# Single-pass rounded-and-remainder score products in the first attention, stacked by groups of batches, scores three steps ahead

## What is computed

```python
def _L0_xattn_ref(x, context, Wq, bq, Wk, bk, Wv, bv, Wo, bo):   # 16 heads of 8 numbers
    q, k, v = heads(x @ Wq.T + bq), heads(context @ Wk.T + bk), heads(context @ Wv.T + bv)
    attn = softmax(einsum('bhnd,bhmd->bhnm', q, k) * HEAD_DIM ** -0.5)
    return merged(einsum('bhnm,bhmd->bhnd', attn, v)) @ Wo.T + bo
x = x + tanh(g_xattn[0]) * _L0_xattn_ref(_layernorm(x), ctx_1024, ...)
x = x + tanh(g_ffn[0]) * _L0_ffn_ref(_layernorm(x), ...)     # 16 experts, top 4, gated
x = x + tanh(g_xattn[1]) * _L1_xattn_ref(_layernorm(x), ctx_1024, ctx_1024, ...)
x = x + tanh(g_ffn[1]) * _L1_ffn_ref(_layernorm(x), ...)     # butterfly up, gelu, butterfly down
```

## Time and profile before

| | |
|---|---|
| time, median of 3 runs (lowest to highest) | 355.55 us (355.16 to 359.48) |
| the profiled execution's own time; its span | 356.27 us; 354.5 us |
| mean granted TensorE clock | 0.986 |
| TensorE matmul busy | 314.1 us, 89% |
| VectorE busy | 240.3 us, 68% |
| ScalarE busy | 211.8 us, 60% |
| GpSimd busy | 159.5 us, 45% |
| DMA packets | 15,091, 27.93 MB |

### The profile page before, as it was taken

The page is one execution under the profiler, slowest core; times in us unless marked ns, Lnnn a source line. Parts: engine busy times, 40 slices in busy tenths (PEclk is TensorE's granted clock), DMA queues, the critical chain, the costliest instruction groups (busy, mean ns, idle before and its releaser), DMA issues.

```text
span 354.5 us, 7313 instructions
## 1 busy us (share of the span) xinstructions
PE 314.1 (89%) x2654; PEld 222.9 (63%) x2654; DVE 240.3 (68%) x603; ACT 211.8 (60%) x411; POOL 159.5 (45%) x254
## 2 busy tenths in 40 slices
PE   4768998839798998999999978999889998999986
PEld 2435777637677776666666645765656665646866
DVE  5672556625566464969998978788958888758251
ACT  3545366615456576685658666668676566764733
POOL 3358998991998021317936340046200394312020
PEclk9999999969899999999999999999999999999999
DMA  7958220120430004323322223413223332000100
GB/s 232 201 70 186 74 66 4 32 35 4 66 121 7 6 2 138 134 89 112 131 93 87 91 88 86 124 46 108 90 92 115 92 108 97 5 1 3 59 31 30
DMA packets 15091, 27.93 MB, mean 79 GB/s; under 512 B 2552, under 2 KB 4040, under 8 KB 15048
## 3 DMA queue, kind: packets, MB, share of 16 engines
q1 hardware_dynamic: 12720, 23.00, 22.2%
q0 software_dynamic: 1408, 3.18, 4.1%
q10 hardware_dynamic: 928, 1.29, 1.3%
HBM read 24.05 MB, written 1.18 MB: 71 GB/s over the span
## 4 chain that ended last, share of the span: by engine, by line
PE 51%; POOL 14%; DVE 13%; issue 8%; ACT 8%; DMA 5%; SPq 1%; ACTq 0%; DVEq 0%; POOLq 0%
PE bank L1116 10%; PE bank L1105 5%; PE bank L1107 5%; PE bank L1106 5%; PE bank L1226 4%; PE bank L931 4%; PE bank L957 3%; PE bank L1211 3%; DMA x_sb<-in_x 3%; DVE rings L1533 3%; DVE rings L1536 2%; POOL xr L442 1%; POOL w_lo L431 1%; DMA rings<-mxr 1%; ACT rings L792 1%
## 5 line engine op out<-in xcount | busy, mean ns | idle before, releaser
L1105 PE MATMUL bank<-xhl,w_hi 128*128 128x512 f32 x128 | 74.9, 585 | 0.8 <-ACT rings L792 0.8
L792 ACT ACTIVATE rings<-bank,cols 128x512 f32<-128x512 f32 x64 | 44.1, 689 | 49.2 <-PE bank L1107 48.9
L1347 DVE TENSOR_REDUCE nt<-bank 128x4 f32<-128x480 f32 x64 | 39.9, 650 | 40.0 <-PE bank L938 40.0
L1533 DVE SCALAR_TENSOR_TENSOR rings<-rings,gates 128x512 f32<-128x512 f32 x64 | 47.4, 740 | 16.9 <-ACT rings L792 16.6
L1107 PE MATMUL bank<-xhl,w_hi 128*128 128x512 f32 x128 | 50.5, 394 | 0.0
L1106 PE MATMUL bank<-xhl,w_lo 128*128 128x512 f32 x128 | 50.3, 393 | 0.0
L931 PE MATMUL bank<-rings,ks 32*120 32x128 f32 x512 | 38.4, 289 | 10.5 <-DMA rings<-rings 6.4
L796 ACT ACTIVATE rings<-bank,b1c 128x512 f32<-128x512 f32 x64 | 44.0, 688 | 0.5
L931 PEld LDWEIGHTS bank<-rings,ks 32*120 32x120 f32 x512 | 32.3, 186 | 15.9 <-issue 12.4
L938 PE MATMUL bank<-ks,rings 32*128 32x120 f32 x512 | 38.9, 291 | 1.3 <-DVE nt L1347 0.7
L1105 PEld LDWEIGHTS bank<-xhl,w_hi 128*128 128x128 f32 x128 | 24.1, 188 | 18.1 <-ACT rings L792 7.9
(11 more groups left out here) (247 smaller groups left out, 625.9 us busy)
## 6 DMA issues: line engine op xcount, KB each, us to landing
gates<-gate_rows SPq DMA_DIRECT2D x64, 256.0 KB, 3.1
bw<-in_L_ffn_w POOLq DMA_DIRECT2D x4, 512.0 KB, 5.3
x_sb<-in_x SPq DMA_DIRECT2D x4, 256.0 KB, 7.7
x_sb<-in_L_ffn_w SPq DMA_DIRECT2D x2, 512.0 KB, 4.3
wide<-in_ctx ACTq DMA_DIRECT2D x4, 240.0 KB, 6.8
out<-xr SPq DMA_DIRECT2D x3, 256.0 KB, 2.1
gates<-in_flies SPq DMA_DIRECT2D x1, 704.0 KB, 7.0
rings<-rings POOLq DMA_DIRECT2D x8, 64.0 KB, 4.5
```

What stands on the lines that cost most here:

```text
L792: act.activation(esg[:, e % 2, :], SB[1 + e % 2][:, :], ACT.Gelu_apprx_sigmoid, bias=b1_in[:, 0, e:e + 1]).then_inc(s["m_sg"], 1)
L1105: pe.matmul(bk[:, :], w1_hi[:, e, branch, :], low(g), start=True, stop=False)
L1347: dve.tensor_reduce(nt[:, b % 2, OF[n], :], score_bank(b, n)[:, 0:HR * M].rearrange("p (r m) -> p r m", r=HR), AX.X, ALU.max, negate=True) ...
L1533: dve.scalar_tensor_tensor(eq[:, j, :], esg[:, j, :], GELU_LIMIT, gates[:, (n - 1) % NG, :], ALU.min, ALU.mult).then_inc(s["m_eq"], 1)
```

## The change

- **Operands.** The score and turned products of the first attention take float32r operands, for which a product is one MATMUL and one LDWEIGHTS. To keep the precision, each of a head's 8 numbers takes four partitions of the 32: for keys the rounded value, the rounded value again, the remainder and (partition `MAX_ROW`) a one; for queries the rounded value, the remainder, the rounded value again and the maximum or zero.
- **Stacks.** A group of four batches has its own slot of keys and of queries. Slots of groups 0 and 1 lie in `w1_lo` and `w1_hi`, those of 2 and 3 in `ks`, `xhl` and `qs`. A slot is filled by three DMAs for keys and three for queries, each to every fourth partition (32 of them); SP issues all, those of groups 2 and 3 between the `mxr` transfers of steps 0 to 3. GpSimd's `stack` is gone.
- **Remainders.** VectorE makes them (`low_keys`, `low_queries`), eight in all, of float32 from the bank and the rounded row.
- **GpSimd.** It fills the slots of groups 2 and 3 with ones (a CAST of 1920 columns each) and zeros (a MEMSET of 2048 columns each). The splits wait for `st_mm` 32 (the end of the turned products of batches 0 to 7), since `w1_hi` and `w1_lo` hold the slots until then; they stand behind the up bias.
- **Order.** Scores run three steps ahead instead of two. Two more half-phases and `turn_max(1)` stand before step 0; maxima are of b+2 and b+3 in step b.

The diff's core. Left out are the renamed calls of the prologue (`phase(-2, 0)` is now `phase(-3, 0)` and so on), the second attention's tiles `p1`, `p1t` and `hid` that move into `mats`, GpSimd's memsets of slots 0 and 1, and on ScalarE the bitcasts to F32R, `turned_max(b + 2)` and its earlier share of the query stacks.

```diff
@@ -57,6 +57,8 @@
+    MAX_ROW = 3
+    AHEAD = 3
@@ -122,7 +124,17 @@
-        qs = ring_row[:, 0:8 * GT].rearrange("p (i r t) -> p i r t", i=2, r=HR)
+        w1_hi_row = w1_hi[:, :, :, :].rearrange("p e j c -> p (e j c)")
+        w1_lo_row = w1_lo[:, :, :, :].rearrange("p e j c -> p (e j c)")
+        KSLOT, QSLOT = HR * GB * M, HR * GT
+        k_rows = (w1_lo_row[:, 0:KSLOT], w1_lo_row[:, KSLOT:2 * KSLOT], ks[:, 0, :], ks[:, 1, :])
+        q_flat = (w1_hi_row[:, 0:QSLOT], w1_hi_row[:, QSLOT:2 * QSLOT],
+                  xhl[:, :, :].rearrange("p s c -> p (s c)"), qs[:, :])
+        k_slot = [v.rearrange("p (r u m) -> p r u m", r=HR, u=GB) for v in k_rows]
+        q_slot = [v.rearrange("p (r u t) -> p r u t", r=HR, u=GB) for v in q_flat]
+        q_lo = ring_row[:, 0:2 * GT].rearrange("p (i t) -> p i t", i=2)
+        k_lo = ring_row[:, 2 * GT:2 * GT + 2 * GB * M].rearrange("p (i t) -> p i t", i=2)
+        kt_row = ring_row[:, 4 * GT:4 * GT + G * GB * M].rearrange("p (g t) -> p g t", g=G)
@@ -234,17 +245,8 @@
-        def stack_k(eng, g, groups):
-            for i in groups:
-                eng.dma_start(ks[32 * i:32 * i + HD, g % 2, :, :],
-                              kt_row[32 * i:32 * i + 32, g, :]
-                              ).then_inc(s[f"ks_ld{g}"], 16)
...
-        def stack_q(eng, g, groups):
-            for i in groups:
-                eng.dma_start(qs[32 * i:32 * i + HD, g % 2, :, :],
-                              q_rows[g][32 * i:32 * i + 32, :]
-                              ).then_inc(s[f"qs_ld{g}"], 16)
+        def stacked(eng, slot, row, src, landed):
+            eng.dma_start(slot[row:P:4].bitcast(F32), src).then_inc(s[landed], 16)
@@ -265,31 +267,46 @@
-            sp.wait_ge(s["ks_fill"], 1)
-            sp.wait_ge(s["kt_rdy"], 1)
-            stack_k(sp, 0, range(HG))
+            def stack_k(g):
+                if g < 2:
+                    sp.wait_ge(s["ks_fill"], g + 1)
+                else:
+                    sp.wait_ge(s["kb_fill"], g - 1)
+                sp.wait_ge(s["kt_rdy"], g + 1)
+                stacked(sp, k_slot[g], 0, kt_row[:, g, :], f"ks_ld{g}")
+                stacked(sp, k_slot[g], 1, kt_row[:, g, :], f"ks_ld{g}")
+                sp.wait_ge(s["kl_rdy"], g + 1)
+                stacked(sp, k_slot[g], 2, k_lo[:, g % 2, :], f"ks_ld{g}")
...
+            def stack_q(g):
+                sp.wait_ge(s["qs_zero"], g + 1)
+                sp.wait_ge(s["qt_rdy"], g + 1)
+                stacked(sp, q_slot[g], 0, q_rows[g], f"qs_ld{g}")
+                stacked(sp, q_slot[g], 2, q_rows[g], f"qs_ld{g}")
+                sp.wait_ge(s["ql_rdy"], g + 1)
+                stacked(sp, q_slot[g], 1, q_lo[:, g % 2, :], f"qs_ld{g}")
...
+            stack_k(0)
...
-            sp.wait_ge(s["qs_zero"], 1)
-            sp.wait_ge(s["qt_rdy"], 1)
-            stack_q(sp, 0, range(HG // 2))
-            sp.wait_ge(s["ks_fill"], 2)
-            sp.wait_ge(s["kt_rdy"], 2)
-            stack_k(sp, 1, range(HG))
+            stack_q(0)
+            stack_k(1)
...
-            sp.wait_ge(s["qs_zero"], 2)
-            sp.wait_ge(s["qt_rdy"], 2)
-            stack_q(sp, 1, range(HG))
+            stack_q(1)
...
-                sp.dma_start(qs[HD:P:32, (b // GB) % 2, :, b % GB * P:(b % GB + 1) * P], mxr[:, b % 2, :]
+                sp.dma_start(q_slot[b // GB][MAX_ROW:P:32, :, b % GB, :].bitcast(F32), mxr[:, b % 2, :]
...
+                if b in (0, 2):
+                    stack_k(2 + b // 2)
+                if b in (1, 3):
+                    stack_q(2 + b // 2)
@@ -423,6 +440,10 @@
+            for g in range(2, G):
+                pool.tensor_copy(k_rows[g], which[:, MAX_ROW:MAX_ROW + 1].to_broadcast([P, KSLOT])).then_inc(s["kb_fill"], 1)
+                pool.memset(q_flat[g].bitcast(F32), 0.0).then_inc(s["qs_zero"], 1)
@@ -433,9 +454,6 @@
-            split(0)
-            split(1)
@@ -451,25 +469,15 @@
-            def stack(g):
-                pool.wait_ge(s["ks_fill"], 2)
-                pool.wait_ge(s["kt_rdy"], g + 1)
-                pool.wait_ge(s["qt_rdy"], g + 1)
-                pool.wait_ge(s["st_mm"], (g - 1) * GB * HG)
-                stack_k(pool, g, range(HG))
-                stack_q(pool, g, range(HG))
-                pool.dma_start(qs[HD:P:32, g % 2, :, :], qs[HD + 1:P:32, g % 2, :, :]
-                               ).then_inc(s[f"qs_ld{g}"], 16)
...
-            stack(2)
-            split(2)
-            split(3)
-            stack(3)
...
+            def halves():
+                pool.wait_ge(s["st_mm"], 2 * GB * HG)
+                for q in range(NQ):
+                    split(q)
@@ -488,6 +496,7 @@
+            halves()
@@ -859,7 +866,7 @@
-                    pe.wait_ge(s["kt_rdy"], g)
+                    pe.wait_ge(s["kl_rdy"], g)
@@ -888,7 +895,7 @@
-                    pe.wait_ge(s["qt_rdy"], g)
+                    pe.wait_ge(s["ql_rdy"], g)
@@ -908,41 +915,39 @@
-                ahead = b + 2
+                ahead = b + AHEAD
...
-                    i, mc, tc = rows_of(b)
+                    k_, q_, u = k_slot[b // GB], q_slot[b // GB], b % GB
...
-                    ia, ma, ta = rows_of(ahead)
+                    ka, qa, ua = k_slot[ahead // GB], q_slot[ahead // GB], ahead % GB
...
-                        pe.wait_ge(s[f"ks_ld{ahead // GB}"], 16 * HG)
-                        pe.wait_ge(s[f"qs_ld{ahead // GB}"], 16 * (HG + ahead // (2 * GB)))
+                        pe.wait_ge(s[f"ks_ld{ahead // GB}"], 16 * 3)
+                        pe.wait_ge(s[f"qs_ld{ahead // GB}"], 16 * 3)
...
-                            mm = pe.matmul(turned_bank(b, gg)[0:M, r * P:(r + 1) * P], ks[32 * gg:32 * gg + 32, i, r, mc],
-                                           qs[32 * gg:32 * gg + 32, i, r, tc], start=True, stop=True)
+                            mm = pe.matmul(turned_bank(b, gg)[0:M, r * P:(r + 1) * P], k_[32 * gg:32 * gg + 32, r, u, :],
+                                           q_[32 * gg:32 * gg + 32, r, u, :], start=True, stop=True)
...
-                            mm = pe.matmul(score_bank(ahead, n)[:, r * M:(r + 1) * M], qs[rows32, ia, r, ta],
-                                           ks[rows32, ia, r, ma], start=True, stop=True)
+                            mm = pe.matmul(score_bank(ahead, n)[:, r * M:(r + 1) * M], qa[rows32, r, ua, :],
+                                           ka[rows32, r, ua, :], start=True, stop=True)
...
-                need(pe, "x1_rdy", b - 3)
+                need(pe, "mxr_rdy", b)
+                need(pe, "x1_rdy", b - 4)
@@ -1045,8 +1050,11 @@
+            phase(-2, 1)
+            phase(-1, 0)
+            turn_max(1)
...
-            pe.wait_ge(s["kt_rdy"], G)
+            pe.wait_ge(s["kl_rdy"], G)
@@ -1058,8 +1066,8 @@
-                if b + 1 < NB:
-                    turn_max(b + 1)
+                if b + 2 < NB:
+                    turn_max(b + 2)
@@ -1275,8 +1283,22 @@
-            keys_of = which[:, HD:HD + 1].unsqueeze(2).to_broadcast([P, HR, GB * M])
-            dve.tensor_copy(ks[:, 0, :, :], keys_of).then_inc(s["ks_fill"], 1)
+            keys_of = which[:, MAX_ROW:MAX_ROW + 1].to_broadcast([P, KSLOT])
+            dve.tensor_copy(k_rows[0], keys_of).then_inc(s["ks_fill"], 1)
...
+            def low_keys(g):
+                dve.wait_ge(s["kt_rdy"], g + 1)
+                if g >= 2:
+                    dve.wait_ge(s[f"ks_ld{g - 2}"], 16 * 3)
+                dve.scalar_tensor_tensor(k_lo[:, g % 2, :].bitcast(F32R), bank[4][:, 0:GB * M], bcol[:, CK0:CK0 + 1],
+                                         kt_row[:, g, :], ALU.add, ALU.subtract).then_inc(s["kl_rdy"], 1)
...
+            def low_queries(g):
+                dve.wait_ge(s["qt_rdy"], g + 1)
+                if g >= 2:
+                    dve.wait_ge(s[f"qs_ld{g - 2}"], 16 * 3)
+                dve.scalar_tensor_tensor(q_lo[:, g % 2, :].bitcast(F32R), bank[2][:, :], bcol[:, CQ0:CQ0 + 1],
+                                         q_rows[g], ALU.add, ALU.subtract).then_inc(s["ql_rdy"], 1)
@@ -1320,16 +1342,24 @@
-            dve.tensor_copy(ks[:, 1, :, :], keys_of).then_inc(s["ks_fill"], 1)
+            dve.wait_ge(s["ld_kb"], 16)
+            low_keys(0)
+            dve.tensor_copy(k_rows[1], keys_of).then_inc(s["ks_fill"], 1)
...
+            low_keys(1)
...
-            for g in range(1, G):
-                normed_rows(g)
+            normed_rows(1)
+            low_queries(0)
+            low_keys(2)
+            normed_rows(2)
+            normed_rows(3)
+            low_queries(1)
+            low_keys(3)
@@ -1421,19 +1451,23 @@
+            low_queries(2)
+            low_queries(3)
...
+            for n in range(HG):
+                maxima(1, n)
...
-                maxima(1, n)
+                maxima(2, n)
...
-                if b + 1 < NB:
-                    maxima(b + 1, HG - 1)
+                if b + 2 < NB:
+                    maxima(b + 2, HG - 1)
...
-                if b + 2 < NB:
```

(3 more changed lines are left out.)

43 lines of the change are left out of this document (19 added, 24 removed).

## The result

The changed kernel takes 369.99 us (median of 4 runs, 369.13 to 372.71); the kernel before, beside it, 357.51 us (4 runs, 355.16 to 360.74). The ratio is 1.0385, with a 95% interval of 1.0275 to 1.0494: slower, where 346.7 us and a gain had been forecast. The profiled execution took 369.65 us, with a span of 367.8.

A forecast was written before the change was run, and what follows sets the result against it. Bound: a step loop through TensorE and VectorE, plus stalls costing 10.2 us. With start +6.4 and 0.44 saved per step, GpSimd binds: mark −9.2, half-phase −0.44, clock +0.8, sum −8.8: 347.4 profiled, 346.7 median; range 342 to 354.

The forecast's parts named there:

- (d): Start: TensorE waits longer before step 0 and its clock is halved after the wait; 0.5 us allowed.
- half chance +0.8: Behind TensorE's wait for GpSimd's router rows: the clock may halve, some 1.7 us in all, taken as +0.8.
- rival B: First attention: TensorE, less busy, loses its clock more than once; two further stretches at 1.7 make 350 us; chance 0.20.
- (a): Start: four VectorE remainder instructions stand ahead of the sums that release GpSimd, 0.65 us each, so 2.6 us.
- (b): Start: VectorE's last remainder waits for group 1's key DMAs, taken at 0.7 us each, a wait of 1.4 us.
- rival E: Cheaper start: remainders lie partly in VectorE's own waits, the clock holds; +4 instead of +6.4, 343.5 us; chance 0.15.
- (c): Before step 0: two more half-phases and four maxima cost 2.4 us, less 0.5 for cheaper prologue products.
- Rival C: Half-phases: single-pass products of 128 columns are no cheaper; the mark moves −3.8, 352 us; chance 0.08.
- F: Stalls: the slot fills wait for something and step 5 still waits as now; 355 us; chance 0.03.
- key DMAs over 2 us: Sign that the forecast is wrong: DMAs stacking keys, taken at 0.7 us each, last longer than 2 us.
- rival D: Stacks: DMAs at 2.2 us each delay GpSimd's head, step 0 and the maxima queued behind; 356.4 us; chance 0.12.
- GpSimd as the next bound: After step 7: GpSimd's splits, values and norm take 29.65 us, router rows ready at 111.7; TensorE waits 1.2 us.

The follow-up runs named there:

- run 1: The changed kernel with score and turned products read as plain float32, two records each again: 359.03 us, ratio to the kernel before 1.0008.
- run 2: The kernel before with only single-pass products (rounded keys, queries and maxima, no remainders, tiles moved for room): 367.21 us, ratio 1.0185.
- run 7: The changed kernel with one unread float32 product per step in steps 2 to 13, using 32 rows of the array instead of 128: 383.32 us.
- Run 11: The changed kernel with five unread float32 products in TensorE's wait for the up matrices, none in the steps: 371.75 us, ratio 1.0372.
- run 3: The changed kernel with one unread float32 product of 256 columns per step in steps 2 to 13: six runs 351 to 358 us, four 384 to 386.
- run 10: The changed kernel with unread products in steps 0 to 13, five more before step 0, and GpSimd's value biases late: 346.75 us, ratio 0.9719.
- run 12: The changed kernel with scores two steps ahead, unread products in steps 0 to 13 and before step 0, late value biases: 345.50 us, ratio 0.9737.

## Why the prediction was wrong

On the scale of the profiled execution the forecast was 347.4 and the time 369.65: 22.2 us. They lie here: step 0 began at 50.63 and not 49.3, +1.3; from step 0 to step 13 passed 75.85 us and not 13 × 4.48 = 58.2, +17.6; from there to the router rows' turn 5.38 and not 4.2 (the 3.0 of TensorE's own mark, 110.5 less 107.5, and the wait of 1.2), +1.2; behind it 235.9 and not 234.0, +2.0. That is 22.1 in all. In the second, the windows show the clock at 0.50; in the first and the last they show it below 1.00 too (0.56 in 40 to 44, 0.54 to 0.88 in 132 to 144).

**The step that failed** is what the forecast gave the clock: (d), "I allow 0.5", the "half chance +0.8" behind the wait, and rival B, which had only "Two further stretches at 1.7". The runs show 0.50 from 56 us to the end of the attention, 6.02 us and so 1.54 more than 4.48 in each step from step 5 on, and 17.6 us in the thirteen steps together. Rival B had named the cause, products of half the records, and got 0.20; its size was wrong by a factor of six to seven (3.4 us against 22). Its reason, that TensorE is "less busy", isn't what the profile shows: TensorE counts as busy for 3.87 of 4.00 us at the low clock. What runs 1 and 2 show is that the kind of product decides; what in it the clock follows is open, with run 7 speaking for the part of the array at work. The row that misled was 22 to 24 at 1.00 with TensorE 0.66 of 2.00 busy. It was read as a clock that bears idle time. Run 11 shows what such a row is worth: 1.00 in 44 to 48, 0.95 in 48 to 52 with step 0 already under way, and 0.50 from 52 on. A short row at 1.00 doesn't show that the clock stays there. The Trainium skill, "TensorE: Matmul & The Clock Gate", Part 1, says that activity releases the throttle and that the throttled state is the default. Run 3 agrees with it, where an extra product in each step went with a clock that came back to 1.00 in six of ten runs; no run shows what counts as activity. The forecast had drawn on this sentence and then weighed it at 3.4 us.

A second omission: what a lower clock does to the bound was priced per product (0.78 for a value pass), not for the step. At 0.50 TensorE alone fills the step (3.87 of 4.00 busy), so its products count one by one, not only those of the chain: in run 7 a filler of 1.11 us made the low step 0.85 us longer, where in run 3, at full clock, at most 0.35 of 0.58 stood on the path.

**The other steps.**

- Start, +6.4 forecast, +7.7 measured. GpSimd's head came at 28.66 (29.3), its up matrices ended at 39.9 (40.5), so (a) and (b) were a little high: 3.4 and not 4.0. At 1.00 step 0 stands at 47.36 (run 10), which is +4.4 and near the +4 of rival E; so some 3.3 us of the +7.7 went with the clock, where (d) allowed 0.5. The third step's prologue, 2.4 in (c), is 1.91 between runs 10 and 12, with the clock at 0.71 in 40 to 42 in run 12. (The 0.5 taken off in (c) was for cheaper products that both runs have, so that 2.4 less 0.5 comes out at 1.9 is luck.)
- Half-phase: 0.65 forecast, 0.60 measured at full clock; the saving of 0.44 was 0.49. Rival C is refuted.
- The step at full clock: 4.48 forecast; 4.61 with a filler that holds at most 0.35 of it. Without the filler some 4.26 is an estimate from these two; no run had such steps at full clock.
- The stalls: gone, as forecast; F is refuted. The page's list of DMA issues (KB each, us from issue to landing), and the stacks of GpSimd in the page of before:

```profile
w_lo<-rings SPq DMA_DIRECT2D x6, 240.0 KB, 3.5
ks<-rings SPq DMA_DIRECT2D x6, 240.0 KB, 2.4
...
w_hi<-qt_row SPq DMA_DIRECT2D x4, 256.0 KB, 2.5
...
rings<-rings POOLq DMA_DIRECT2D x8, 64.0 KB, 4.5
```

A stack of 240 KB takes 2.4 to 3.5 us from issue to landing, so the sign "key DMAs over 2 us" came true to the letter. The harm that rival D added up didn't come: GpSimd's head stood at 28.66 and not 4.7 behind 29.3, and in the steps of runs 10 and 12, at full clock, TensorE waits for no stack and at most 0.2 us for maxima. So D is refuted. "SBUF — State Buffer", section "Door 1: The DMA port swizzle", of the Trainium skill says that the rate of a DMA depends on how many ports its partitions reach. The landing times agree, 240 KB sooner than 64 KB; issuer and number of DMAs at once differ too, so they don't prove it.
- GpSimd as the next bound: it did not bind in the changed kernel. At full clock it does. From the end of step 7 to the router rows 31.3 us (83.70 to 115.03, run 3) where 29.65 was forecast, the fetches being waited for twice (0.86 and 1.06 against 0.5 in all), and TensorE waited 2.43 against 1.2.
- The end: the tail had been taken over from before, with 0.8 for a low clock; it took 2.0 more, with the clock below 1.00 until 144.

That the kernel of run 10 has a median of 346.75, next to the 346.7 of the forecast, proves no term: it has fillers, products at the start and late biases that the change has not.

## What to carry to other kernels

This is one kernel's lesson. Before a change takes work off TensorE, ask what will hold its clock there. A busy share near 1 is no answer: it was 3.87 of 4.00 here at half clock. The number of passes of each product is what changed, and the granted clock must be read for the windows after the change, not before it. Where single-pass products replace float32 ones in a chain with waits, budget a whole part at half clock as one case, price it per step with TensorE as the bound, and try unread products in the waits, at the entry and in each step, before giving up the change.
